# Two layers of masked graph attention on one core: seeds of the masks laid across chunk boundaries, the rows of s turned later, and the last normalisation by row tile

## The reference

```python
# layer 0: x (4096, 64), adj (4096, 4096) of 0 and 1, E = entity_embs (4096, 64)
scores = ((x @ W0) @ a1)[:, None] + ((E @ W0) @ a2)[None, :]
e = where(scores > 0, scores, 0.2 * scores); e = where(adj > 0, e, -9e15)
h = softmax(e, axis=1) @ E + x
x = layernorm(x + elu(h))
# layer 1: the same adjacency
wh = x @ W1
e = leaky_relu((wh @ s1)[:, None] + (wh @ s2)[None, :], 0.01)
out = softmax(where(adj > 0, e, -1e9), axis=1) @ wh + bias
x = layernorm(x + out)          # the result, (4096, 64)
```

## Time and profile before

| | us |
|---|---|
| median of three executions | 628.15 (627.94 to 630.33) |
| the profiled execution | 629.13 |
| its span, first to last instruction | 627.3 |
| PE, DVE, ACT, POOL busy | 504.5, 560.3, 541.8, 169.6 |
| granted TensorE clock, mean | 0.975 |
| chunk 0 begins its exponentials | 46.42 |
| chunk 1 | 101.98 |
| chunk 2 | 176.66 |
| chunk 3 | 252.87 |
| chunk 4 | 322.52 |
| chunk 5 | 369.62 |
| chunk 6 | 412.11 |
| chunk 7 | 472.92 |
| chunk 8 | 535.06 |
| chunk 9 | 591.04 |
| last DVE instruction ends | 624.91 |

### The profile page before, as it was taken

How to read it: one execution, slowest core, us unless ns; L and a number is a source line. 1 busy time by engine, 2 the same in 40 slices (tenths; PEclk the granted TensorE clock), 3 DMA queues, 4 the chain that set the end, 5 groups by cost and what they waited for, 6 DMA issues and landing times.

```text
span 627.3 us, 14309 instructions
## 1 busy us (share of the span) xinstructions
PE 504.5 (80%) x6039; PEld 235.7 (38%) x6039; DVE 560.3 (89%) x781; ACT 541.8 (86%) x627; POOL 169.6 (27%) x105
## 2 busy tenths in 40 slices
PE   1316777889989799999989786789898888989994
PEld 1213444333444334434346452343333333333352
DVE  4998999999979998989978979959998998899795
ACT  1878994989999999799989889989897999778883
POOL 1070100276024670167101001005510523024051
PEclk9999788899999999999998899989999999999998
DMA  8998995667477666460010010000010001000001
GB/s 176 398 377 325 360 308 192 238 235 269 150 234 272 230 226 233 138 222 6 16 39 2 1 36 2 15 22 1 2 26 18 1 1 33 3 1 1 18 3 26
DMA packets 21340, 76.16 MB, mean 121 GB/s; under 512 B 10412, under 2 KB 11612, under 8 KB 13084
## 3 DMA queue, kind: packets, MB, share of 16 engines
q1 hardware_dynamic: 20472, 74.89, 34.5%
q0 software_dynamic: 112, 0.28, 0.2%
q10 hardware_dynamic: 692, 0.08, 0.1%
HBM read 74.16 MB, written 1.09 MB: 120 GB/s over the span
## 4 chain that ended last, share of the span: by engine, by line
DVE 35%; issue 26%; ACT 18%; PE 15%; DMA 3%; POOL 2%; POOLq 0%; ACTq 0%; DVEq 0%
DVE junk L946 19%; ACT Pm L814 12%; DVE zps L1104 9%; PE acc L1225 8%; PE zps L1286 4%; DMA adj_in<-in_adj 3%; DVE v L923 2%; ACT zps L806 2%; ACT v L672 2%; PE acc L1232 2%; ACT u_row L688 1%; DMA acol<-in_L_gnn_a 1%; PE zps L1195 1%; DVE tot L1015 0%; DVE tot L1010 0%
## 5 line engine op out<-in xcount | busy, mean ns | idle before, releaser
L814 ACT ACTIVATE Pm<-zps,ebias 128x1024 f32<-128x1024 f32 (+1 forms) x320 | 292.3, 934 | 41.0 <-DVE zps L1104 35.9
L806 ACT ACTIVATE zps<-S_row,ntau_col 128x1024 f32<-128x1024 f32 (+1 forms) x211 | 200.6, 954 | 5.6
L1286 PE MATMUL zps<-D,v 128*128 128x128 bf16 x2048 | 165.2, 224 | 36.9 <-ACT zps L806 22.4
L1286 PEld LDWEIGHTS zps<-D,v 128*128 128x128 fp8e4 x2048 | 119.1, 100 | 176.2 <-ACT zps L806 91.2
L1225 PE MATMUL acc<-Pm,VE 128*32 128x512 f32 (+2 forms) x1280 | 148.2, 536 | 21.0 <-ACT Pm L814 12.8
L1225 PE MATMUL acc<-Pm,X 128*32 128x512 f32 (+2 forms) x1280 | 138.8, 519 | 26.4 <-ACT Pm L814 22.6
L946 DVE CUSTOM_DVE_ANT_0 junk<-v,adj_in 128x2048 int8<-128x2048 int8 (+3 forms) x88 | 155.9, 1807 | 0.0
L946 DVE CUSTOM_DVE_ANT_0 junk<-v,u_row 128x2048 int8<-128x2048 int8 x64 | 155.4, 2441 | 0.2
L1104 DVE SCALAR_TENSOR_TENSOR zps<-S_row,tau_col,zps 128x1024 f32<-128x1024 f32 (+1 forms) x109 | 112.4, 1054 | 38.9 <-PE zps L1286 38.4
L1232 PE MATMUL acc<-Pm,ones 128*32 128x256 f32 (+1 forms) x1280 | 87.6, 346 | 0.0
L549 POOL TENSOR_TENSOR tAB<-flag,totW 128x520 f32<-128x520 f32 (+1 forms) x7 | 11.7, 1670 | 224.4 <-PE zps L1286 116.2
(11 more groups left out here) (170 smaller groups left out, 250.9 us busy)
## 6 DMA issues: line engine op xcount, KB each, us to landing
adj_in<-in_adj SPq DMA_DIRECT2D x62, 1024.0 KB, 5.3
S_row<-S_rows_scratch SPq DMA_DIRECT2D x6, 512.0 KB, 4.1
Pm<-in_adj SPq DMA_DIRECT2D x2, 1024.0 KB, 10.6
VE<-in_L_gnn_entity_embs SPq DMA_DIRECT2D x2, 512.0 KB, 5.9
S_row<-S_rows_scratch SPq DMA_DIRECT2D x3, 256.0 KB, 3.1
out<-tAB SPq DMA_DIRECT2D x3, 256.0 KB, 2.6
adj_in<-u_row_scratch SPq DMA_DIRECT2D x2, 256.0 KB, 3.7
S_row<-S_rows_scratch POOLq DMA_DIRECT2D x1, 256.0 KB, 6.8
```

The costliest lines, as they stand in the source:

```text
L806: a.activation(mask_of(n), S_row[:, C % 2, 0:R(C) * P], ACT.Relu, bias=ntau_col[:, layer(C), n % JT:n % JT + 1]).then_inc(seed_done, 1)
L814: a.activation(Pm_of(k, 0, R(C) * P), mask_of(k), ACT.Exp, bias=ebias[:, layer(C), int(seeded(k)), J:J + 1])\
L1286: last = t.matmul(mask[:, r * P:(r + 1) * P], v[:, chunks[C][1] + r, J * P:(J + 1) * P], D[:, C % 2, PART * second + r, :], start=(r * P % ...
```

## The change

- The plan of seeds: around narrow chunks (0 to 1, 3 to 4, 4 to 5, 5 to 6) a seed may take a bank whose last user was a step of the chunk before, or the spread "u". So three steps at the start of chunk 1, one in chunk 4, two in chunk 5 and two in chunk 6 can be seeded at step 0. The unseeded steps are spread anew or listed (`WITHOUT`): chunk 1 unseeded at 7, 27, 28; chunk 4 at 0, 2, 4, 7, 8, 29; chunk 5 at 2, 4, 8, 25, 28, 31; chunk 6 at 1, 4, 7, 8, 10, 13, 16, 19, 22, 24, 27, 30. The other chunks keep their lists. In all 213 steps are seeded instead of 211.
- The rows of s of chunks 3 and 4 are turned by PE 3 steps after the spread of u (24 instead of 21, 20 instead of 17), and ACT saves them at step 25 and 21 instead of 18 and 14.
- Behind a narrow chunk PE leaves its last two products for after the masks of steps 0 and 1 of the next.
- Row maxima of layer 1 in chunk 4 stand at 0 and 1 and no longer at 15 and 16 (`EARLY`), and the late ones begin at step 23 instead of 22.
- The end of the last chunk is a function of its own, `finish_last`, by row tile: product with rden and sum in one instruction, `bn_stats` and `bn_aggr` for mean and variance, subtraction and scale in one.

```diff
-SEEDS = ((29, 28, 28, 26, 24), (28, 20, 20, 10, 0))
+SEEDS = ((29, 28, 28, 26, 24), (32, 20, 20, 10, 0))
+    S_BEHIND = 3
-    EARLY = (3, 4, 5, 7, 11, 12, 15, 16, 17, 18, 19)
-    LATE_AT = 22
+    EARLY = (0, 1, 3, 4, 5, 7, 11, 12, 17, 18, 19)
+    LATE_AT = 23
+    WITHOUT = {1: (28,), 4: (0, 2, 4), 5: (2, 4, 28, 31)}
...
+        def rows_at(C):
+            return at("rows", C) + S_BEHIND * (C - 1 in SPREAD) if at("rows", C) else None
...
-                    if J == at("rows", C):
-                        users += [("u", C - 1)] * (C - 1 in SPREAD) + [("rows", C - 1)]
+                    users += [("u", C - 1)] * (C - 1 in SPREAD and J == at("rows", C))
+                    users += [("rows", C - 1)] * (J == rows_at(C))
...
-            first = JT * C if C == LAST or not narrow(C) and C != NC + 1 else 0
-            may = [k for k in range(JT * C + 2 * (first < JT * C and C < NC), JT * (C + 1)) if (users_before["step", k] or C == 0)
-                   and all(what == "step" and m >= first for what, m in users_before["step", k])]
+            across = C != LAST and (narrow(C) or narrow(max(C - 1, 0)))
+            may = [k for k in range(JT * C, JT * (C + 1)) if (users_before["step", k] or C == 0)
+                   and all(what == "u" or what == "step" and m >= JT * C * (not across) for what, m in users_before["step", k])]
             n = min(SEEDS[layer(C)][C - FIRSTS[layer(C)]], len(may))
-            seeded_steps |= {k for i, k in enumerate(may) if (i + 1) * n // len(may) > i * n // len(may)}
+            if across and C:
+                without = [may[(2 * i + 1) * len(may) // (2 * (len(may) - n))] % JT for i in range(len(may) - n)]
+                seeded_steps |= {k for k in may if k % JT not in WITHOUT.get(C, without)}
+            else:
+                seeded_steps |= {k for i, k in enumerate(may) if (i + 1) * n // len(may) > i * n // len(may)}
...
-            free = max((m + 1 for what, m in users_before["step", k]), default=0)
+            free = max((m + 1 if what == "step" else JT * (m + 1) + at("rows", m + 1) - ROWS_LEAD
+                        for what, m in users_before["step", k]), default=0)
...
-                        if layer(C - 1) == 0 and J == at("rows", C) + (1 if C - 1 not in SPREAD else -ROWS_LEAD):
-                            if C - 1 in SPREAD:
-                                save_spread_u(C - 1)
+                        if C - 1 in SPREAD and J == at("rows", C) - ROWS_LEAD:
+                            save_spread_u(C - 1)
+                        if layer(C - 1) == 0 and J == rows_at(C) + 1:
                             save_rows(C - 1)
...
-            add_up(dve, d, link, LAST)
-            normalise(dve, d, link, LAST, sums, squares)
-            scale(dve, d, LAST)
+            finish_last()
...
-                while C and narrow(C - 1) and next_product < JT * C:
+                while C and narrow(C - 1) and next_product < JT * C - 2:
...
-                        if J == at("rows", C):
-                            if C - 1 in SPREAD:
-                                spread_u(C - 1)
+                        if C - 1 in SPREAD and J == at("rows", C):
+                            spread_u(C - 1)
+                        if J == rows_at(C):
                             turn_rows(C - 1)
```

More of the change, by code:

```diff
@@ L152, in build @@
         um = sb("um", [P, 3, RT, Q])
+        stats, moments = sb("stats", [P, PART, 6]), sb("moments", [P, PART, 2])
         um_known = sb("um_known", [P, PART])
@@ L1017, in squares @@
                     .then_inc(var_done, 1)
+            def finish_last():
+                C, n = LAST, R(LAST)
+                xs, h, tAf, tBf = tiles_of(C)
+                dve.wait_ge(proj_done, C + 1)
+                link(d.tensor_tensor(tA[:, 0:n, :], flag[:, C % 2, 0:n].unsqueeze(2).broadcast_to([P, n, F1]),
+                                     totW[:, :].unsqueeze(1).broadcast_to([P, n, F1]), ALU.mult))
+                dve.wait_ge(o_saved, C + 1)
+                link(d.tensor_tensor(o[:, 0:n, :], o[:, 0:n, :], tA[:, 0:n, :], ALU.add))
+                link(d.reciprocal(rden[:, 0:n], o[:, 0:n, F]))
+                for r in range(n):
+                    last = d.scalar_tensor_tensor(tBf[:, r, :], h[:, r, :], rden[:, r:r + 1], xs[:, r, :], ALU.mult, ALU.add)
+                link(last)
+                for r in range(n):
+                    last = d.bn_stats(stats[:, r, :], tBf[:, r, :])
+                link(last)
+                for r in range(n):
+                    last = d.bn_aggr(moments[:, r, :], stats[:, r, :])
+                link(last)
+                d.tensor_scalar(var[:, 0:n], moments[:, 0:n, 1], LN_EPS, None, ALU.add).then_inc(var_done, 1)
+                dve.wait_ge(rstd_done, C + 1)
+                for r in range(n):
+                    last = d.tensor_scalar(tBf[:, r, :], tBf[:, r, :], moments[:, r, 0:1], rstd[:, r:r + 1],
+                                           ALU.subtract, ALU.mult)
+                last.then_inc(new_done, 1)
             def scores(C):
```

## The result

| | median us | runs (lowest to highest) |
|---|---|---|
| before | 628.39 | 22 (625.68 to 630.78) |
| changed | 626.11 | 22 (624.02 to 629.09) |

The ratio is 0.9965, interval 0.9954 to 0.9975: 2.3 us less, and inside the 0.5% that the prediction counted as no change. The forecast was 623.2. The sign was right; less than half of the size came.

What follows compares the result with a forecast made beforehand. No engine was taken to be full (DVE 89%, ACT 86%, PE 80%); the time was lost at chunk boundaries. Gains of 3.3 + 1.25 + 0.4 = 4.95 us from the median 628.15 gave 623.2 us, range 619.8 to 627.8.

Steps and rivals of the forecast that it cites:

- Part A: Chunk 0 to chunk 1: three seeds ahead of step 0 remove ACT's waits for maxima; 3.3 us gained, bounds 0 and 5.7.
- rival 1: Start of chunk 1: DVE sets chunk 2's diagonals, so only 1.5 us of that gain survives; 625.0 us, chance 0.18.
- The price of the products: Start of chunk 1: two products held behind masks delay the save of the sums; new ACT wait near 1 us.
- the prediction's chain: Start of chunk 1: ACT free at 96.98, seeds end 100.2, exponential 0 at 100.45, exponential 3 at 108.3, before 111.72.
- Part B: Chunk 4: 26 seeds for 24, waits for maxima at steps 24 to 26 go; -0.7 us, bounds -2.0 and +1.5.
- Part C: Chunk 4 to 5 and chunk 5, into chunk 6: earlier exponentials 0; chunk 6's DVE waits worked out as 4.1 and 2.7 us.
- B and C together: Chunks 4 to 6: 1.25 us gained, carried into chunk 7; bounds -1.5 (a loss) and +3.5.
- Rival 2: Reordering costs (chunk 4's later spread, chunk 5's step 31, small end instructions) win; 627.2 us, chance 0.15 including no effect.
- Rival 3: Start of chunk 1: two half-clock PE stretches vanish, 1.5 us each; 620.5 us, chance 0.08.
- Part D: End of the last chunk by row tile: 3.2 us for 3.56, 0.4 gained; bounds -3.5 (a loss) and +2.3.
- rival 4: Boundaries and spreads: idle PE brings more half-clock stretches, 1.5 us lost in each; 632.2 us at six more, chance 0.07.

Runs made afterwards that it cites:

- e3_products: Changed kernel with all products of a narrow chunk again ahead of the next masks, at three boundaries: 622.84 us, 0.9916 of the kernel before.
- e9_rows: Changed kernel with the rows of s turned and saved in their old place again: 625.41 us, 0.9958 of the kernel before.
- e10_maxima: Changed kernel with chunk 4's row maxima back at steps 15 and 16, late ones from 22: 626.2 us, 0.9971 of the kernel before.
- the copy: Changed kernel run and traced again without edit: 625.55 us, 0.9953 of before; the kernel before was likewise repeated: 625.89 us, 0.9965.
- e1b_old6: Changed kernel with only chunk 6's old list of unseeded steps put back, second timing, two executions: 621.7 us, 0.9893 of the kernel before.
- e2_seed31: Changed kernel with step 31 of chunk 5 seeded: 624.66 us, 0.995 of the kernel before.
- e4_old_end: Changed kernel with the old ending of the last chunk, four row tiles at once: 627.7 us, 0.9985 of the kernel before.
- e11_old1: Changed kernel with chunk 1's old list, unseeded at 0, 1, 2, 7, 27: 631.51 us, 1.005 of the kernel before.

## Why the prediction was right or wrong

**Part A, right in size.** Forecast 3.3; 3.3 from the medians of the two kernels, 3.5 from the stretches above. The three seeds, the removed wait and DVE's slack before the diagonals were as told, so rival 1 fell. The price of the products was right at full clock only: a wait near 1 us was forecast before the save of the sums; it is 2.1 to 2.5 in the five traces with a half-clock stretch there, and 0.5 to 1.0 in the five without. That holding them back costs more than it gives (e3_products) the forecast did not see. The start of the prediction's chain also came out right (exponential 0 3.27 after the last one, forecast 3.47).

**Part B, better than forecast.** Chunk 4 with its handover: 2.4 us for a forecast of 2.0 (exponential 0 of chunk 5). ACT no longer waits for the maxima of steps 24 to 26, the 0.2 of the s rows is gone (e9_rows: 0.1), the spread makes ACT stand 1.3 for 0.9. The row maxima at steps 0 and 1, counted as what saves the spread, cost 0.4, and ACT's wait for the spread is 1.4 without that move (e10_maxima): they saved 0.1 of it.

**Part C, the step that failed.** Up to exponential 0 of chunk 6 it held: step 31's maximum made ACT wait 1.33 (forecast 0.65), and chunk 6 began 235.45 - 233.63 = 1.8 us earlier after chunk 2 than before. The failed step is "Chunk 6, though, is DVE's: it waits twice at the start, 7.1 us, and then not again [...] has the same 12 maxima, and I work out waits of 4.1 and 2.7 us." That DVE sets the chunk was right. The waits were not: DVE waits six times, 9.0 us in all: 3.71, 2.36, 0.89, 0.26, 1.18 and 0.66. The first two came much as worked out (6.1 us, and 6.9 in the copy, for 6.8); the four behind them, 3.0 us, stood in no sum. I counted the maxima and not their distances: 4, 7, 8 and 13 come up on DVE before PE has their masks, and so does 30 near the end. With step 31's maximum, 0.7, DVE needs 2.6 us more from diagonals to diagonals, and it had come to the first of them only 1.2 us earlier after chunk 2 than before (230.05 for 231.25). The far end is no part of it: ACT stands 2.77 before exponential 0 of chunk 7, for 1.4 before, but that exponential follows its diagonals after 2.3 us in both. Forecast for B and C together 1.25 gained, measured 1.4 lost (297.65 us from chunk 2 to chunk 7 for 296.26): 2.65 us, all of the miss in the part that can be read trace against trace, and 2.2 of it are the waits (9.0 for 6.8). e1b_old6 confirms it: with that list alone 3.9 us come back, and DVE's waits are 4.0 us shorter. How much of the four later waits is the list and how much PE's clock stays open; by the two traces of the changed kernel the clock's part is some 0.5 us (an estimate, 1.18 less 0.66).

Rival 2 named this kind of end, with the price at step 31 and in the spread. They cost 0.7 (e2_seed31) and 0.4; the price of 3.2 was in a place that no rival had. Rival 3's 620.5 is off by its own terms: the forecast's 623.2 less twice 1.5 is 620.2.

**Part D, right.** Forecast 3.2 for 3.56; measured 2.13 + 0.98 = 3.11, and the end is 0.4 shorter, gone in e4_old_end. One row tile's product and sum 0.22 (forecast 0.19), stats 0.15 (0.15), aggregation 0.10 (0.10), scale 0.25 (0.25). The estimate from the Trainium skill, "VectorE: DVE Perf Modes", section "The TRN2 errata", 3.6 us for the sixteen without overlap, does not hold here: they take 0.87 + 0.60 + 0.38 + 0.98 = 2.83, 0.18 each. Taken one by one their lengths add up to 3.8 us (a product with its sum is 0.28 long, and the next starts 0.20 later), so it is the overlap that the estimate left out.

**Rivals 3 and 4, the clock.** Besides the one at the end of each trace, the granted clock is half in seven stretches of the profiled kernel before, in four of the changed one, and in four of either's copy: neither rival is a matter of the change as a whole. But one place is in part. In both traces of before such a stretch begins 1.9 to 2.5 us after exponential 0 of chunk 1, with the products ahead. In five of ten traces with the changed order of products one begins between 97.8 and 99.5 us, around that exponential, and there the way from chunk 0 to chunk 2 takes 75.6 to 76.4 us; in the other five it takes 74.0 to 75.0. In the three traces with the new list and the products ahead there is none in that place. So a stretch there costs about 1.6 us, in half of these executions, which is rival 4's price. That the held-back products cause it is not shown: three traces without are few, and PE had stood 1.95 to 2.79 us before the first masks in the five with a stretch and 1.65 to 2.48 in the five without. The Trainium skill, "TensorE: Matmul & The Clock Gate", Part 1, says that the cold phase differs from run to run of one kernel; the two traces of each kernel agree, with stretches from 67.9, 81.5, 98.6 and 429.7 us in one of the changed kernel, and from 98.1, 214.2, 347.3 and 405.3 in the other.

**Range and chances.** 626.11 lies inside 619.8 to 627.8, which was wide enough to take in rival 2's end; the forecast's own 4.95 us came only as 2.3. "Faster by over 0.5%" had 0.67 and "within 0.5%" 0.24; the second came.

## What to carry to other kernels

A seed laid ahead of a chunk's first step shortens the boundary where the engine that writes it stands idle for a maximum (chunk 1: 3.3 us). In a chunk that DVE bounds it puts ACT's work ahead of DVE's first maximum, and two lists with the same number of maxima differed here by 3.2 us through their first four steps: write out DVE's sequence with the masks it needs, wait by wait, before calling a list equal. Compare traces chunk by chunk, and find out first in which part two executions of one kernel differ; here it was nearly all ahead of chunk 2, and larger than the gain.

## What the runs showed that I had not expected

- Two executions of the kernel before differ by 4 us in their first 175 us (176.7 and 172.6 to chunk 2, in each of them several half-clock stretches between 66 and 132 us) and by less than 0.1 in the following 450; the two of the changed kernel differ by 0.3 there.
- Statistics and aggregation (BATCH_NORM_STATS2, BATCH_NORM_AGGREGATE) cost 0.15 and 0.10 us a row tile of 64 elements, in groups of four.
- A half-clock stretch costs where PE is waited for: 1.6 us at the start of chunk 1 (five traces against five), but nothing in chunk 6 of the kernel before (60.8 us with one from 415.1, 60.8 in its copy without). e11_old1 has 6.8 us at half clock from 408.8, and the longest chunk 6 of all, 65.8.
